# Inverting 16 row sums per position instead of 256, with the spreading to 256 columns on ScalarE

## The reference

```
# third layer: 16 heads of 16 columns
scores = einsum(q, k) / 4;  scores = where(mask == 0, -1e9, scores)
e      = exp(scores - max(scores)) * mask
probs  = e / (sum(e) + 1e-9)
attn   = einsum(probs, v);  out = attn @ Wo.T + bo;  x = layernorm(out + residual)
# fourth layer: 16 heads of 16 columns
attn   = softmax(where(xa_mask, -big, q @ k * scale)) @ v
x      = x + attn @ proj_w + proj_b;  x = x + gelu(layernorm(x) @ fc1 + b) @ fc2 + b
```

## Time and profile before

| | |
|---|---|
| time, median of 3 runs | 1362.54 us (1361.63 to 1363.40) |
| the profiled execution | 1361.59 us, its span 1359.8 us |
| busy, of the span: TensorE, its weight loads | 94%, 76% |
| VectorE, ScalarE, GpSimd | 78%, 50%, 41% |
| chain that ended last: TensorE, VectorE, issue | 67%, 20%, 3% |
| granted TensorE clock, mean | 0.994 of full |

### The profile page before, as it was taken

One profiled execution on the slowest core, in us unless ns is written; L12 is line 12 of the kernel. 1 busy time (PEld: TensorE's weight loads), 2 busy tenths in 40 slices (PEclk: granted clock), 3 DMA queues, 4 the chain that ended last, 5 costly groups with the idle time before them and its releaser, 6 DMA issues.

```text
span 1359.8 us, 25054 instructions
## 1 busy us (share of the span) xinstructions
PE 1272.6 (94%) x9539; PEld 1036.5 (76%) x9539; DVE 1058.6 (78%) x2140; ACT 683.2 (50%) x1509; POOL 564.3 (41%) x696
## 2 busy tenths in 40 slices
PE   7899999998899999999999999999999999999987
PEld 6789988766677777777777777777777777777766
DVE  4677873678788888888888767788888888888883
ACT  4567776223554544555544433554444555555543
POOL 4644432014444454435444311544444444454541
PEclk9999999998999999999999999999999999999999
DMA  4521223010000000000010100000000000000000
GB/s 126 115 86 59 75 83 112 1 14 2 20 24 1 9 1 9 25 1 1 1 36 8 44 2 20 16 11 1 5 24 10 1 1 17 13 5 1 1 10 16
DMA packets 48472, 34.23 MB, mean 25 GB/s; under 512 B 22177, under 2 KB 45536, under 8 KB 48352
## 3 DMA queue, kind: packets, MB, share of 16 engines
q1 hardware_dynamic: 48304, 32.59, 8.6%
q10 hardware_dynamic: 48, 0.01, 0.0%
HBM read 23.26 MB, written 8.39 MB: 23 GB/s over the span
## 4 chain that ended last, share of the span: by engine, by line
PE 67%; DVE 20%; issue 3%; ACT 3%; POOL 3%; DMA 2%; SPq 1%; ACTq 0%; DVEq 0%; POOLq 0%
PE ps L875 7%; PE ps L968 7%; PE ps L979 7%; PE ps L911 7%; DVE zt L1420 6%; PE ps L860 6%; PE ps L932 5%; PE ps L850 5%; PE ps L816 5%; PE ps L918 4%; PE ps L799 3%; DVE mx L1388 2%; PE ps L1075 2%; PE ps L907 2%; DVE mx L1399 2%
## 5 line engine op out<-in xcount | busy, mean ns | idle before, releaser
L1624 POOL TENSOR_TENSOR rstd<-mv,halfneg 128x1 f32<-128x1 f32 x192 | 105.5, 551 | 432.7 <-DVE mv L1357 432.4
L850 PE MATMUL ps<-wk,tt 128*128 128x308 f32 x512 | 145.3, 425 | 1.8 <-ACT tt L1175 0.9
L968 PEld LDWEIGHTS ps<-tt,fc 128*128 128x128 f32 x1024 | 117.8, 192 | 12.4 <-ACT tt L1172 9.9
L968 PE MATMUL ps<-tt,fc 128*128 128x128 f32 x1024 | 124.6, 278 | 0.9 <-ACT tt L1172 0.9
L1196 ACT ACTIVATE pr<-pr 128x616 f32<-128x616 f32 x128 | 91.3, 715 | 62.8 <-POOL pr L1663 37.0
L1663 POOL TENSOR_TENSOR front<-mx,front 128x616 f32<-128x616 f32 x64 | 79.1, 1237 | 98.4 <-DVE mx L1388 98.2
L850 PEld LDWEIGHTS ps<-wk,tt 128*128 128x128 f32 x512 | 93.4, 190 | 33.4 <-issue 3.3
L1172 ACT ACTIVATE tt<-ps,cols 128x128 f32<-128x128 f32 x192 | 76.8, 453 | 81.5 <-PE ps L799 80.5
L1420 DVE RECIPROCAL zt<-mx 128x256 f32<-128x256 f32 x64 | 111.6, 1743 | 0.6
L1637 POOL TENSOR_TENSOR xt<-xt,row_bo 128x256 f32<-128x256 f32 x96 | 70.7, 740 | 85.6 <-PE ps L799 50.1
L1453 DVE TENSOR_TENSOR xt<-xt,ps 128x256 f32<-128x256 f32 x160 | 65.2, 409 | 51.4 <-PE ps L932 25.0
(11 more groups left out here) (221 smaller groups left out, 3025.4 us busy)
## 6 DMA issues: line engine op xcount, KB each, us to landing
out_dram<-xt SPq DMA_DIRECT2D x64, 128.0 KB, 1.8
xt<-in_x_dram SPq DMA_DIRECT2D x32, 128.0 KB, 2.3
xt<-out_dram SPq DMA_DIRECT2D x32, 128.0 KB, 2.2
fc<-in_L_xattn_fc_w_dram SPq DMA_DIRECT2D x2, 1024.0 KB, 8.0
wk<-in_L_xattn_wkv_dram SPq DMA_DIRECT2D x4, 512.0 KB, 6.8
front<-in_L_xattn_wkv_dram SPq DMA_DIRECT2D x4, 512.0 KB, 4.3
wo<-in_L_xattn_wo_dram SPq DMA_DIRECT2D x1, 1024.0 KB, 5.7
kb<-in_L_xattn_wq_dram SPq DMA_DIRECT2D x1, 1024.0 KB, 5.5
```

The lines of the kernel that those rows point to most:

```text
L850: last = mm(bank(lane, k)[:, SFROM[k]:SFROM[k] + HB * KEYS], t[:, lane, kc, :], wk[:, kc, b, h0:h0 + HB * KEYS], start=kc == 0, stop=kc == ...
L968: last = mm(bank(lane, c // 4)[:, c % 4 * P:(c % 4 + 1) * P], fc1[:, kc, c * P:(c + 1) * P], t[:, lane, kc, :], start=kc == 0, stop=kc == ...
L1624: p.tensor_tensor(rstd[:, n:n + 1], mv[:, n, 1:2], halfneg[:, :], ALU.pow).then_inc(done["rstd"], 1)
```

## The change

The reciprocal of the third and fourth attention's sums is taken on the 16 sums alone, into the small tile `rec`. A new step `widen` on ScalarE waits for it and copies the 16 numbers, each repeated 16 times by a step of zero, to the 256 columns of `zt`. `rturn` waits for `widen` where it waited for `recip`. The fifth chunk's copies (`pturn_rest`) are VectorE's as before. All five strings of `TURNS` are replaced: apart from the 64 steps more on ScalarE, each engine makes the same steps in another order, in the first phase too.

```
-    return steps + [("den_eps", a.name)] * (a is L2) + [(s, a.name) for s in ("recip", "rturn", "rec_t", "mix", "heads", "proj", "resid")]
+    return steps + [("den_eps", a.name)] * (a is L2) + [(s, a.name) for s in ("recip", "widen", "rturn", "rec_t", "mix", "heads", "proj", "resid")]
...
-    "scalar": ("item_act", "turned", "query_bias", "expo", "pturn_main", "rec_t", "u_sb", "gelu", "w2_sb", "wqt_sb", "k1_sb", "vt_sb", "silu", "more_act"),
+    "scalar": ("item_act", "turned", "query_bias", "expo", "pturn_main", "widen", "rec_t", "u_sb", "gelu", "w2_sb", "wqt_sb", "k1_sb", "vt_sb", "silu", "more_act"),
...
     "sync": (
-        "0aaa120aaaaa3aa2aa31aaaaaaaa0011aa2332010312aaaaa23a01a20133220121003302211a30a3aaa0213213aa32113030aa2120aaa0a0"
-        "32101b132122213002b0331001bb31b1220333b2023120130032310121022133"),
+        "3212aaaa3aaa0a0aa1aaaaa11aa02aa0aa23a30aa0113322001aa122332aa002110aa03323132aa110a10aa33a22aa2322a121103a10003a"
+        "ab2b33321000123311010220b110bb222b103330233120011231030213220133"),
...
             def rturn(key, run):
                 lane = run.lane
-                pe.wait_ge(done["recip"], at("recip", key, run))
+                pe.wait_ge(done["widen"], at("widen", key, run))
                 pe.wait_ge(done["pturn_rest"], at("pturn_rest", key + ".1", run))
...
+            def widen(key, run):
+                act.wait_ge(done["recip"], at("recip", key, run))
+                src = rec[:, run.lane, :, :].rearrange("p g h -> p (g h)").unsqueeze(2).to_broadcast([P, 2 * HG, L2.hd])
+                ac(z[:, run.lane, 0:H].rearrange("p (h d) -> p h d", d=L2.hd), src, ACT.Copy).then_inc(done["widen"], 1)
...
                 else:
-                    dst = z[:, lane, 0:H].rearrange("p (h d) -> p h d", d=L2.hd)
-                    src = mx[:, lane, :, :].rearrange("p g h -> p (g h)").unsqueeze(2).to_broadcast([P, 2 * HG, L2.hd])
+                    dst, src = rec[:, lane, :, :], mx[:, lane, :, :]
                 v.reciprocal(dst, src).then_inc(done["recip"], 1)
```

More of the change, by code:

```diff
@@ L231 @@
     "tensor": (
[L232 to L240, removed]
@@ L276 @@
-    "gpsimd": (
[L277 to L282, removed]
+        "iiiiiiii201ii2iii0ii1i01iii2iiii0ii1ii0i2i0230130123001203012311230123130233120103231201230013010312312013220233"
@@ new lines @@
+        "0312003202131021001230003123221023031131202131211023110230331203102202031323223012221031300123302131203103302103"
+        "332012311201320020213101032031232231231011312322012313233231221132332323233332323333"),
+    "vector": (
+        "iii202011201iiii31010iiii302321ii002ii00222000011112033211123122103032303333131300001221100120130322110321213233"
+        "1303022322310330100022001323001122031111123233312222100233301310003012210011200303122232112211233312300233033110"
+        "0321002011100201032322111211232002233302113333300013221010020002222113311101321033233203233320003011000212303102"
+        "111122211302033122130322330320331122131123022000311123312223333sssssssssssssssassasaasassasaaasasaaassasaaasasaa"
+        "asaaaasaasaasssasaa000aa0222111133230011300000110000203111230111122100222100222210010100010320001033001303123131"
+        "3301000100000112101321001010232122121110202020011211222200212211131303300002233300001210211321233203233233112332"
+        "2322001001311130110121331300002222330130003023200333013122112221222212003331313010120100101110331101200003322233"
+        "1311123233032030122011202311222210021211312333000003200002330232113112321320232333113323022202110011133310131100"
+        "1202302202133003300023002033133122201221202221333210113101320100110011301130100202332332333331001222300222113012"
+        "1122221120210231113100002303220200033303213111320312223333133213222020110033111033001101100223231220000303310002"
+        "2331333122202201122221013200031013131200311111301310002013233233213323311322202112112113222212211211333222323132"
+        "23223233bbbbb3b3333323bb3bbbbbbbb2bbbb2bbbb2bbb3bbb2bb3bb0000113112330220211200000310000103322113101111220100022"
+        "2310330300003100000110001222320023330311011112000313001111021100102032233333212222120303321311201220203111212001"
+        "1131233030000220000023123131211332231032233313203322320200111111113122203010002032331303303000203020333131112222"
+        "2100021232232001331310120100111011131302002033223331233332231101222001132121122002212200131131000203302200001133"
+        "0211331222330223333232233023211001011331111011303012022230332010300300230020333113222222110022212101111033333000"
+        "1200111101131320002033221133312333300022321210012213121222002212311113000332200003300212031213323110322333231132"
+        "3032222001013311130130111212032000332231303000022030331031221122200111222202113031330320010101113310121000222033"
+        "333133332322222111132112221212212311133312232323333222322303333332222213333333333333323"),
@@ new lines @@
+    "scalar": (
+        "iiiiiii2i10ii012iiii01i0i221033012030031201311023212130233213030100231011203222133032102313200102311012031221033"
+        "2320301200313211012022311302332013020031101123022121302320313000323103021312013322131202310003201031123122231331"
+        "022312331022103aaa3asaaassaaaasasasaassaasaaasaaasasaaasaasaasaassssssssssssssssss011320000113001201221002010011"
+        "3001213010032000102120201122210113310213231100230332321220203123012231001003302333113202133012121100310020203110"
+        "3200221332112211103302123031301023332210220233211021200313003023331100322133211201110300002230123010322312221310"
+        "31110221301120303223330120221332100220303103013321301032213302112010100130221033210230213212211113322131b1233bbb"
+        "22bbbb332322bbbbbbbb33222031120330003301011203010100023330102210131101020032010123202032212311011133102320110230"
+        "2312333022023203112210010303302331132031033122012011010003221310232032031221211311032210011302330322322302013320"
+        "1122103013300023331120031232311201100100032211033220032132211203113102123103102303233210220233201102201310330033"
+        "2131032021133201211030120020311022303232212131311102233132332232211233233333322333"),
@@ new lines @@
+    "gpsimd": (
+        "ii201ii323i0000011221112233330a00101122332231030011212301223a300013212103221330000131122233123300010121213233320"
+        "0011211322033012223330a10112203000001111100000300111102212202110302222131323321233332023010030320000331111103230"
+        "011121102221102032222133330221123330320100330232000001331111203011121002232211012223221133233021133303b203000332"
+        "2000021310011103311110022132221122232132123323333322031301320000203000301111030101112100222211130222321213330232"
+        "1033332032000213300000331111201033111100222221110222220313323311233303200203310320000331110110203311121022221100"
+        "10222213323132321333322010030033200010331111200033111210222121122222031333322333132233333"),
@@ L1293, in more_act @@
                     act.sem_inc(more_r, MORE)
-            steps = {"item_act": item_act, "turned": turned, "query_bias": query_bias, "expo": expo, "pturn_main": pturn_main, "rec_t": rec_t, "u_sb": u_sb,
+            steps = {"item_act": item_act, "turned": turned, "query_bias": query_bias, "expo": expo, "pturn_main": pturn_main, "widen": widen, "rec_t": rec_t, "u_sb": u_sb,
                      "gelu": gelu, "w2_sb": w2_sb, "wqt_sb": wqt_sb, "k1_sb": k1_sb, "vt_sb": vt_sb, "silu": silu, "more_act": more_act}
```

43 lines of the change are left out of this document (10 added, 33 removed).

## The result

The changed kernel takes 1310.68 us (median, 1310.27 to 1311.70) against 1362.97 us for the one before: a ratio of 0.962, 95% interval 0.960 to 0.964, so 52 us less. The prediction was 1322.5 us, 40 us less, with a range of 1304 to 1352.

The account below looks back on a forecast made before the run. In the second phase TensorE and VectorE were both near full, with TensorE stalled for VectorE's wide reciprocal. TensorE's 35.3 us plus 5 us credited to VectorE gave 40 us less: 1322.5 us, range 1304 to 1352.

Parts of the forecast that it names:

- What bounds the kernel: Second phase: TensorE 94% and VectorE 82% busy; `rturn`'s weight loads stood 52.3 us for the wide reciprocal, 8.4% of the chain.
- The two prices: Reciprocal 16 wide on VectorE 251 ns instead of 1743; ScalarE's widening copy of 256 columns 0.41 us, bounds 0.38 and 0.60.
- The hand-over: Reciprocal to `widen` and `widen` to `rturn`: 0.04 us each; `rturn` ready after 0.74 us instead of 1.78.
- VectorE's relief: The narrower reciprocal relieves VectorE of 1492 ns, 64 times, 95 us in all.
- ScalarE's queue: `widen` in ScalarE's order is delayed 0.14 us, leaving a gain of 0.9 us for each reciprocal.
- TensorE's side of the sum: The 46 stalls ahead of `rturn` each shrink by 0.9 us or go away if shorter: 35.3 us.
- VectorE's side: Chain places in VectorE's order gain 1.49 us each, 28 us for 19; 5 us credited beyond TensorE's 35.3.
- rival (b): The whole chain in the second phase is given back: 59 us, 1302.5 us; chance 0.11 for below 1308.
- The first 320 us: First stretch, new order on all engines with nothing removed: 0 gain, 5 us on both sides.
- (a): Another wait takes the place of the old; each stall shrinks by 0.5 us: 22 us less, 1340.5 us; chance 0.19.
- (c): ScalarE's queue holds `rturn` back; break-even at 1.04 us mean lateness, at 1.4 us slower: 1379 us; chance 0.07.
- The signs that were named: Changed profile: `rturn` waits for ScalarE under 17 us, TensorE idle about 25, VectorE busy about 960, reciprocal off the chain's head.

Follow-up runs that it names:

- VectorE's load back: Changed kernel with two unread reciprocals of 88 columns added on VectorE behind each narrow one: 1337.6 us, ratio 0.981.
- The late kernel: Changed kernel with ScalarE's widening copy made three times, each after the one ahead: 1334.5 us, ratio 0.979.
- the one with the early reciprocal: Changed kernel with the addition of 1e-9 and the reciprocal moved on VectorE to right behind the second group's sum: 1317.0 us, ratio 0.966.
- two kernels with the late result: Changed kernel with ScalarE's widening copy made three times, 1334.5 us, or twice, 1321.8 us.

## Why the prediction was right, and where it was off

**What bounds the kernel** held. The step that it named, TensorE's stall ahead of `rturn` and the reciprocal's places on the chain, is gone from both views, and the time with it.

**The two prices** held to a few ns: 251 ns predicted and 243 measured for the reciprocal of 16 sums, 413 and 415 ns for the copy on ScalarE with a step of zero. The hand-over of 0.04 us was right. For the copy the Trainium skill's table ("VectorE: DVE Perf Modes", the section on the TRN2 errata) gave 400 ns as an estimate, and the rows of the trace were nearer. Its rule that small pieces pay a fixed latency each is seen in the 8 or 16 columns that take 201 and 243 ns; it didn't decide, since 240 columns of reciprocal cost six times that.

**VectorE's relief** was to be 95 us; the busy time fell by 91.0 (1058.6 to 967.6).

**ScalarE's queue** held as the prediction had it. `widen` starts 0.13 us after the end of its reciprocal on the mean, 0.04 of that the hand-over, so the queue costs 0.09 us where 0.14 were predicted; 53 of the 64 start within 0.1 us, and the latest 1.7 us after. ScalarE stands 31.5 us ahead of `widen` for the reciprocal, and has time to.

**TensorE's side of the sum** was 35.3 us, for 0.9 us on each of 46 stalls. The 0.9 us was right: with the 0.79 us from the start of the reciprocal to the end of the copy and the hand-over of 0.04, `rturn` is ready after 0.83 us on the mean instead of 1.78, so 0.95 us earlier. The price was too high: being 0.91 us late costs 23 us, 0.45 us costs 11, so 0.95 us are worth some 24 us, an estimate from these two runs. The waits themselves fell by 48.3 us (52.3 to 4.0), more than predicted; in the old order 20.1 us of them are left. So the term was too large as time, by some 11 us, while as waiting it was too small.

**VectorE's side** is the term that was sized wrong the other way. The prediction worked out that 19 places of the chain went on in VectorE's order, at 1.49 us each 28 us, then credited 5 us of it, arguing that TensorE's idle time of 58.8 us was the limit of both together. The run with VectorE's load back lost 26 us for 65 of the 91 us of busy time. That limit was no reason to take off 23 us: the 52 us gained are less than 58.8, only 39.5 of them came out of idle time, and 11.6 out of busy time. The full chain, 59 us, was called rival (b) with 0.11; the result lies between it and the forecast, 12 us from the forecast and 8 from the rival. The two terms were off in opposite directions, so the sum of 40 us came nearer to the 52 than its parts deserve; that much is luck.

**How the two gains add up** is open. The two losses, 26 and 23 us, sum to 49, but the first run put back 65 of 91 us. At its last rate of 0.5 the remaining 26 us would cost 14 more, so that the two sides would be some 40 and 24 us, 64 together (an estimate that goes past what was tried), against 54 for the old code in the new order. So both are real gains of 20 us and more, and some 10 us may be counted in both. No run had the two together in part.

**The first 320 us** were to give 0, with 5 us on both sides: the first `rturn` came 1.07 us earlier, and that is its own reciprocal.

**Rivals.** (a), another wait in the place of the old one, did not come true: of the waits of TensorE's weight loads for another engine the two that grew most are both L875's, for VectorE's weighing in the second attention (2.2 to 6.4 us) and for GpSimd (1.0 to 4.1), together 7.3 us against 48.3 that went. (c), ScalarE's queue, needed a mean lateness above 1.04 us. The late kernel with 0.91 us shows that such a delay does cost time, 23 us of it; the changed kernel's is 0.09.

**The signs that were named**: `rturn` under 17 us of waiting (4.0), TensorE's idle time in the second phase about 25 us (22), VectorE busy about 960 us (967.6), no reciprocal at the head of the chain. All came so, within 8 us.

## What to carry to other kernels

An instruction that an in-order engine executes on the way to a busy one has two prices, the time until its result is there and the time it takes from its own queue. Read both off the chain: the places where it goes to the waiter, and those where it goes to the next of its own engine. Take neither for nothing, and don't cap their sum at the idle time of the engine that waits: here 11.6 of 51.1 us came out of its busy time. The full sum is too much all the same (59 us by the chain, 52 measured). And do the costly operation on the distinct values before they are repeated: the copy with a step of zero took 0.42 us on ScalarE and 0.38 on VectorE here, against 1.74 us for 256 reciprocals.

## What the runs showed of the hardware

**GpSimd holds up some operations of VectorE.** An addition to 16 columns on VectorE takes 166 ns by the median and up to 1211 ns, in the changed kernel as in the one before (1209); reciprocals of the same 16 columns never take over 254 ns. Of the changed kernel's tile `mx` (min, median, max, first and last start):

```profile
L1412 DVE TENSOR_SCALAR mx<-mx x32: 110/166/1211, 318.9 to 1269.0; 128x16 f32<-128x16 f32 x32
```

and of its tile `rec`:

```profile
L1424 DVE RECIPROCAL rec<-mx x128: 186/204/254, 288.7 to 1290.6; 128x8 f32<-128x8 f32 x64, 128x16 f32<-128x16 f32 x64
```

The longest addition in order of time, with what GpSimd did (rows of other engines left out):

```profile
1006.20 1.22 POOL L1667 TENSOR_TENSOR front<-mx,front 128x616 f32<-128x616 f32 x1 [0.52 <-DVE mx L1393]
1006.24 1.21 DVE L1412 TENSOR_SCALAR mx<-mx 128x16 f32<-128x16 f32 x1
```

GpSimd's operation ends at 1007.42 us and the addition at 1007.45. It is so each time: 4 of 32 additions take over 200 ns in the changed kernel, 8 in the one before and 15 in the one with the early reciprocal, and each of these 27 started while GpSimd was at an operation on two tiles (L1667 or L1641 here) and ended 0.03 us after it. The reciprocal isn't held: 5 of 64 lie wholly within such an operation and take at most 247 ns. A copy of 256 columns is. In the kernel that spreads on VectorE:

```profile
L1428 DVE COPY zt<-rec x64: 293/295/1252, 318.9 to 1296.9; 128x256 f32<-128x256 f32 x64
```

The 13 of these that take over 400 ns all end 0.15 us after an operation of GpSimd. The median of the copy is 295 ns, less than ScalarE's 415.

The Trainium skill ("Perfetto Trace Analysis", the section on optimizing Scalar and DVE operations) says that GpSimd shares an SBUF port with VectorE and that some of VectorE's operations take it exclusively. The traces agree in that the held operation goes on only when GpSimd's ends; that the port is what it waits for, no run here shows.

**The clock.** The granted clock of TensorE was 0.83 of full in some stretches of 10 us in both kernels (in the changed one from 60 to 70 us and from 440 to 450). At the start of the second phase, before (the columns of the earlier trace rows):

```profile
310.00:320.00 10.00, 7.98 (x39) 5.39 (x37) 9.54 (x16) 3.35 (x7) 6.50 (x5) 0.83 0.01 2
```

and after:

```profile
310.00:320.00 10.00, 8.53 (x51) 5.50 (x50) 8.95 (x17) 5.54 (x11) 6.36 (x5) 1.00 0.01 2
```

The mean over the span is 0.994 before and 0.997 after. Full speed is 2.4 GHz and the level of the slow parts 1.2 GHz. The 0.003 between them times 1309 us is 4 us of full speed, an estimate from these rows. Executions of one and the same kernel say nearly as much: of 31 of the kernel before, the 9 with a granted clock of 0.991 and 0.992 took 1364.7 us on the mean, the 11 with 0.995 to 0.997 took 1360.9, so about 1 us for each 0.001. Against the latter the changed kernel (1311.3 us on the mean of 9, at 0.996 and 0.997) is still 50 us faster. So some 3 of the 52 us go with the clock; whether the change brought the higher clock about, no run shows. The old order with the new code has 0.994 in its trace and is 5 to 6 us slower than the changed kernel, so some 3 us of what the new order adds may be this. The traces of the two kernels with the late result have 0.999, and those kernels are slower all the same.
